# First attention: a decayed state per head in place of four of ten blocks

## The reference

```python
lam = exp2(-8 * (1..16) / 16)                      # one decay per head
scores = einsum('bhid,bhjd->bhij', q, k) * diag    # exp(-lam*(i-j)) for i >= j, else 0
o_intra = einsum('bhij,bhje->bhie', scores, v)
o_inter = einsum('bhid,bhde->bhie', q * q_dec, kv) # q_dec = exp(-lam*(r+1))
kv = exp(-lam*CHUNK) * kv + einsum('bhjd,bhje->bhde', k * k_dec, v)
o = o_intra + o_inter
```

## Time and profile before

| | us |
|---|---|
| median of 3 runs | 4115.63 (4114.98 to 4118.08) |
| the profiled execution's own time | 4116.67 |
| its span, first to last instruction | 4114.9 |
| PE busy | 3815.0 (93%) |
| DVE busy | 2393.4 (58%) |
| ACT busy | 1449.7 (35%) |
| POOL busy | 1332.2 (32%) |

### The profile page before, as it was taken

One profiled execution on the slowest core, in us unless ns is written; L12 is line 12 of the kernel. 1 busy time (PEld: TensorE's weight loads), 2 busy tenths in 40 slices (PEclk: granted clock), 3 DMA queues, 4 the chain that ended last, 5 costly groups with the idle time before them and its releaser, 6 DMA issues. The chain is left out here.

```text
span 4114.9 us, 51894 instructions
## 1 busy us (share of the span) xinstructions
PE 3815.0 (93%) x19048; PEld 2746.2 (67%) x19048; DVE 2393.4 (58%) x3950; ACT 1449.7 (35%) x2205; POOL 1332.2 (32%) x1674
## 2 busy tenths in 40 slices
PE   6877999999999999999999999999999999978678
PEld 5755777677767776677767776677767776664423
DVE  5644556555654666556654666456654665465347
ACT  4422342424243433424242433334242433314124
POOL 2421452235312541235313541244213541121114
PEclk9989999999999999999999999999999999987789
DMA  6456533254424433254324533354324433332304
GB/s 234 171 186 245 189 133 139 83 196 158 144 68 179 164 133 127 86 215 147 129 88 154 181 116 135 105 202 138 123 98 180 164 126 105 113 105 73 133 12 153
DMA packets 173802, 579.03 MB, mean 141 GB/s; under 512 B 14728, under 2 KB 14984, under 8 KB 168175
## 3 DMA queue, kind: packets, MB, share of 16 engines
q1 hardware_dynamic: 169854, 568.37, 38.8%
q10 hardware_dynamic: 3696, 7.34, 0.5%
HBM read 490.19 MB, written 84.93 MB: 140 GB/s over the span
## 5 line engine op out<-in xcount | busy, mean ns | idle before, releaser
L1776 PE MATMUL ps_P<-XnT_hi,w_ring 128*128 128x512 f32 x3328 | 1079.6, 406 | 51.6 <-DVE silu L1445 25.7
L1776 PEld LDWEIGHTS ps_P<-XnT_hi,w_ring 128*128 128x128 f32 x3328 | 610.0, 191 | 215.2 <-issue 76.2
L1776 PE MATMUL ps_P<-XnT_lo,w_ring 128*128 128x512 f32 x1664 | 659.0, 396 | 0.0
L1435 DVE TENSOR_REDUCE row_max<-ps_T 128x2 fp32r<-128x768 f32 (+3 forms) x448 | 399.3, 915 | 248.8 <-PE ps_T L1932 238.7
L833 POOL TENSOR_TENSOR pT_lo<-pf,pT_hi 128x512 fp32r<-128x512 f32 x320 | 410.8, 1291 | 303.7 <-ACT pT_hi L971 299.2
L1085 ACT ACTIVATE probs<-ps_E 128x1024 f32<-128x1024 f32 x320 | 327.1, 1022 | 393.2 <-PE ps_E L1947 393.2
L909 POOL TENSOR_TENSOR hT_lo<-hf,hT_hi 128x512 fp32r<-128x512 f32 x128 | 164.3, 1284 | 921.1 <-ACT hT_hi L971 921.1
L851 POOL TENSOR_SCALAR_AFFINE_SELECT probs<-probs 128x512 f32<-128x512 f32 x256 | 159.5, 635 | 652.1 <-ACT probs L1085 651.1
L1776 PEld LDWEIGHTS ps_P<-XnT_lo,w_ring 128*128 128x128 f32 x1664 | 317.6, 191 | 71.4
L1776 PE MATMUL ps_Y<-w_big,hT_hi 128*128 128x512 f32 x896 | 331.5, 416 | 23.0 <-POOL hT_lo L909 11.0
L824 POOL TENSOR_TENSOR sines<-swapped,sinT 128x512 f32<-128x512 f32 x160 | 213.2, 1332 | 348.7 <-ACT swapped L971 342.8
(11 more groups left out here) (307 smaller groups left out, 7263.5 us busy)
## 6 DMA issues: line engine op xcount, KB each, us to landing
w_ring<-split_dram SPq DMA_DIRECT2D x412, 512.0 KB, 3.4
w_big<-split_dram SPq DMA_DIRECT2D x64, 2048.0 KB, 7.8
dec<-decay SPq DMA_DIRECT2D x32, 1024.0 KB, 4.9
split_dram<-w_ring SPq DMA_DIRECT2D x58, 512.0 KB, 4.3
split_dram<-w_big SPq DMA_DIRECT2D x36, 512.0 KB, 4.4
wo1w<-split_dram SPq DMA_DIRECT2D x8, 2048.0 KB, 7.5
gatew<-split_dram SPq DMA_DIRECT2D x7, 2048.0 KB, 10.9
x_dram<-X SPq DMA_DIRECT2D x8, 1024.0 KB, 5.4
```

The lines of the kernel that those rows point to most:

```text
L1435: last = dve.reduce_max(row_max[:, g % 2, block, heads_of(ns)].rearrange("p (b n) -> p b n", n=len(ns)), psT[:, :, at:at + len(ns) * w].re ...
L1776: last = pe.matmul(dst, stat[s_], mov[m_], start=first_ and k == 0, stop=last_ and k == n - 1)
```

## The change

The ten blocks of a group become six score products and a state. The first two key tiles leave the state: keys (not transposed; `keys_back` turns them back through PE) times values that were scaled by their decay to the end of tile 1 (`scaled_values`). The queries of tiles 2 and 3 are multiplied with the state (`state_product`), the decay since the boundary is applied (table `far`), and the result is added to their own blocks. Score products are regrouped: tile j with the query tiles of its own pair, two heads at a time (parts 0 and 1), and the diagonal block of the second tile for four heads (part 2). The raw weights of pass 0 are staged in other memory, and the pieces of the group's output weights are split at other places. The decay table keeps its size.

```diff
+NJOB, NRING, SCORES, INTER = 10, 8, range(2, 8), (8, 9)
+def score_job(k): return divmod(k - SCORES[0], 3)
+P_F = {k: n for n, k in enumerate((0, 1, 2, 3, 4, 5, "state", 6, 7, 8, 9, "sum0", "sum1"))}
+P_HI = {k: n for n, k in enumerate((0, 1, 2, 3, "state", 4, 5, 6, 7, 8, 9))}
+UNIT_AT, KEYS_AT = (0, 1, 2, 3, 5), 4
-            out["blk", g, k + (2 if g == 0 else 7)] = [("w", BIG_O + g, k)]
+            out["blk", g, k] = [("w", BIG_O + g, k)]
...
 # ScalarE, rope, after the loop over u
+                act.wait_ge(*proj.need(n, g, KEYS_AT))
+                copy(kv[0][:, :], ps["Y0"][:, :]).then_inc(*rope_hi.hit(n, g, KEYS_AT))
                 rope_high(n, g, NU - 1)
+            def values_high(n, t):
+                act.wait_ge(*vals.need(n, t))
+                if t < 2:
+                    if t == 0 and n >= 2:
+                        act.wait_ge(*x3_out.need(n - 2))
+                    copy(v32[:, t, :], ps[YB[t % 2]][:, :])
+                copy(v[0][:, t, :], ps[YB[t % 2]][:, :]).then_inc(*v_hi.hit(n, t))
             def blocks(n, g):
+                for k in range(NJOB):
+                    if k == 4:
+                        act.wait_ge(*pv.need(n, g, 1))
+                        copy(kv[0][:, :], ps[PB[g % 2]][:, :]).then_inc(*p_hi.hit(n, g, P_HI["state"]))
+                    if k == 6 and g == 0:
+                        values_high(n, 2)
+                        values_high(n, 3)
+                    if k == 7:
+                        ...
+                        act.wait_ge(*pv.need(n, g, 4))
+                        for h in range(2):
+                            copy(oT[0][:, 2 * h:2 * h + 2, 0:2 * P], ps[EB[h]] ...).then_inc(*o_hi.hit(n, g, h))
+                    if k < NRING: ... copy(pT[0][:, k % 4, :], pf[:, k % 2, :]) ...
+                    else: ... wait sum{h}; copy(oT[0][:, 2 * h:2 * h + 2, 2 * P:4 * P], pf[:, k % 2, :]) ...
+                    if n == 0 and k >= 6:
+                        first(("blk", g, k - 6))
 # VectorE
             def blocks(n, g):
+                for k in range(2):
+                    if g == 0:
+                        values_low(n, k)
+                    scaled_values(n, g, k)         # pf <- v32 * k_dec, both in SBUF
+                if g:
+                    accumulate(n, g - 1, 0)
+                    accumulate(n, g - 1, 1)
                 dve.wait_ge(*dec_in.need(n, g))
+                for k in range(2, 6):
+                    scaled_scores(n, g, k)         # pf <- bank T * dec; waits for p_lo of job k-2
+                    if g == 1 and n:
+                        measure_pc(n - 1, k - 2)
+                dve.wait_ge(*p_hi.need(n, g, P_HI["state"]))
+                low(kv[1][:, :], ps[PB[g % 2]][:, :], kv[0][:, :]).then_inc(*p_f.hit(n, g, P_F["state"]))
+                for t in range(2, NT):
+                    accumulate(n, g - 1, t) if g else values_low(n, t)
+                for k in (6, 7):
+                    scaled_scores(n, g, k)
+                    if n == 0 and k == 6:
+                        first(("blk", g, 0))
+                for h in range(2):
+                    dve.wait_ge(*o_hi.need(n, g, h))
+                    low(oT[1] of heads 2h, 2h+1, tiles 0 and 1, ps[EB[h]] ...).then_inc(*o_lo.hit(n, g, h))
+                if n == 0:
+                    first(("blk", g, 1))
+                for k in INTER:
+                    scaled_scores(n, g, k)
+                for h, k in enumerate(INTER):
+                    dve.wait_ge(*pv.need(n, g, NRING - 1))
+                    dve.tensor_tensor(pf[:, k % 2, :], ps[EB[h]][:, :], pf[:, k % 2, :], ALU.add) ... sum{h}
+                    if n == 0:
+                        first(("blk", g, 2 + h))
 # TensorE
+            def keys_back(n, g):
+                pe.wait_ge(*rope_lo.need(n, g, 0))
+                dst = fill("Y0", rope_hi.need(n, g, KEYS_AT))
+                for t in range(2):
+                    for s_ in range(2):
+                        last = pe.matmul(dst[:, cols(2 * t + s_)], kT[s_][:, cols(t)], identr[:, :], start=True, stop=True)
+                last.then_inc(*proj.hit(n, g, KEYS_AT))
+            def state(n, g):                       # 2 tiles x 3 matmuls 128x512 into PB[g % 2]
+            def score_product(n, g, k):            # 3 matmuls 128x512
+            def value_product(n, g, k):            # parts 0, 1: 3 of 128x512 into EB[part], filled
+                dst = fill(EB[part], p_f sum{part} if pair else o_lo.need(n, g, part))
+                ...                                # part 2: 6 of 128x256, 3 into each of E0 and E1
+            def state_product(n, g, k):            # 6 matmuls 128x256 into TB[k % 2]
             def blocks(n, g):
                 pe.wait_ge(*rope_lo.need(n, g, NU - 1))
+                for k in range(2, 6):
+                    score_product(n, g, k)
+                if g == 0:
+                    all_values(n, 2)
+                state(n, g)
+                if g == 0:
+                    all_values(n, 3)
+                else:
+                    output(n, g - 1, 2)
+                    output(n, g - 1, 3)
+                value_product(n, g, 2)
+                value_product(n, g, 3)
+                score_product(n, g, 6)
+                score_product(n, g, 7)
+                value_product(n, g, 4)
+                for k in INTER:
+                    state_product(n, g, k)
+                for k in range(5, 8):
+                    value_product(n, g, k)
 # TensorE, the main loop
                         for u in range(NU):
                             project(n, g, u)
+                            if u == 3:
+                                keys_back(n, g)
...
-                            for t in range(NT):
+                            for t in range(2):
                                 all_values(n, t)
```

More of the change, by code:

```diff
@@ L175 @@
 assert len(PIECES) == NUNITS == len(set(PIECES))
+MOVED = sum(len(at) for key, at in FIRST.items() if key[0] != "slot")
 INDEX = {p: r for r, p in enumerate(PIECES)}
@@ L694, in _ @@
                         big(n, BIG_O + g)
-                        for k in range(NBLK + LAG + 1):
+                        for k in range(4):
                             if n == 0:
@@ L1524, in _ @@
                                     measure_qb(c, t)
[L1525 to L1526 removed]
+                            if c >= 0:
+                                for t in range(NT):
                                     norm("qb", c, t, y_acc[:, t, :], y_acc[:, t, :])
[L1528 to L1532 removed]
                         blocks(n, g)
@@ L1775, in product @@
                     for s_, m_ in ((0, 0), (1, 0), (0, 1)):
-                        last = pe.matmul(dst, stat[s_], mov[m_], start=first_ and k == 0, stop=last_ and k == n - 1)
+                        last = pe.matmul(dst, stat[s_], mov[m_], start=first_ and k == 0, stop=last_ and k == n - 1, **kw)
                         k += 1
@@ L1826, in output @@
                     big_ready(n, BIG_O + g)
-                pe.wait_ge(*o_lo.need(n, g, t))
+                pe.wait_ge(*(o_lo.need(n, g, 1) if t < 2 else p_lo.need(n, g, INTER[1])))
                 dst = fill(YB[t % 2], wo_acc.need(n, g, t))
                 product(dst[:, :], [(halves(oT, h, cols(t)), big_w(WB, h)) for h in range(HG)]).then_inc(*wo.hit(n, g, t))
+            def score_product(n, g, k):
+                pair, part = score_job(k)
+                dst = fill(TB[k % 2], p_f.need(n, g, P_F[k]))
+                at = slice(2 * pair * P, 2 * (pair + 1) * P) if part < 2 else cols(2 * pair + 1)
+                h = heads_of_part(part)
+                product(dst[:, :].rearrange("p (h i) -> p h i", h=h.stop - h.start),
+                        [(halves(kT, cols(2 * pair + part // 2)), halves(qT, h, at))]).then_inc(*score.hit(n, g, k - 2))
@@ new lines, in state @@
+            def state(n, g):
+                dst = fill(PB[g % 2], p_f.need(n, g, P_F["state"]))
+                keys = kv[0][:, :].rearrange("p (t s d) -> p t s d", t=2, s=2)
+                for t in range(2):
+                    pe.wait_ge(*p_lo.need(n, g, t))
+                    product(dst[:, :], [([keys[:, t, s_, :] for s_ in range(2)], halves(pT, t, slice(None)))], t == 0, t == 1)\
+                        .then_inc(*pv.hit(n, g, t))
+            def value_product(n, g, k):
+                pair, part = score_job(k)
+                j = 2 * pair + part // 2
+                if g == 0:
+                    pe.wait_ge(*v_lo.need(n, j))
+                pe.wait_ge(*p_lo.need(n, g, k))
+                stat, mov = halves(v, j, cols(g)), halves(pT, k % 4, slice(None))
+                if part < 2:
+                    dst = fill(EB[part], p_f.need(n, g, P_F[f"sum{part}"]) if pair else o_lo.need(n, g, part))
+                    last = product(dst[:, :], [(stat, mov)], True, False, skip_group_check=True)
+                else:
+                    for h in range(2):
```

(12 more changed lines are left out.)

202 lines of the change are left out of this document (105 added, 97 removed).

## The result

The changed kernel takes 4206.2 us (median of 4, 4198.8 to 4208.8) against 4116.9 beside it: ratio 1.0214, interval 1.0197 to 1.0232. The forecast was 4135 with a range to 4160. The direction held; the size did not: 89 us instead of 18.

A forecast was written before the change was run, and what follows sets the result against it. PE, busy 93% of the span, was taken to bound the kernel. From 4116.7 us, the walks gave -5.5 and falls of the clock +24: 4135, slower; range 4100 to 4160.

The forecast's parts named there:

- The matmul count: PE's matmul slots per group: 36.0 us after the change, 2.1 us less per group, 67 us over 32 groups.
- the new wait: Before output 0 of the previous group, PE waits for ACT's copy emptying bank Y0, 2.8 us.
- T: The end of projection 4 on PE, from which the prediction counts times within a group.
- the walk of all three kinds of group: Queue-by-queue timing: group 0 27.75 us against 28.79, group 1 +0.2 against 40.85, steady group 40.25 against 40.18.
- The clock: PE's granted clock falls behind the new gaps: 21 x 0.6 x 1.4 plus 7 x 0.8 x 1.2, +24 us, bounds 0 to 45.
- with no falls: Rival at the gap before output 0: clock stays at 2.4 GHz, not slower, 4111 us; chance 0.25.
- The next group's first sine waits for its swap until 30.5: just covered: At a steady group's end, POOL's last low halves end about 30.6 us from T; +1.0 us if they push that sine.
- The rival that named POOL: POOL's last two low halves push the next group's sines: +1.0 us in 28 groups, all falls, 4169 us; chance 0.15.
- The moves of the decay load and the prefetches cost nothing: The next group's whole projection phase covers them: a 1 MB load against 25 us until first use.
- If I were wrong about Y0: Without the bank wait, PE would stand before job 2's decay instead; the group would win back only about 0.5 us.
- Scaled values: DVE jobs reading two SBUF tiles: 0.69 us each in steady groups, 1.1 and 1.27 in group 0.
- Sequence 0: Pass 0, with weight splits moved and later constants: taken as 0 us, bounds -15 and +12.

The follow-up runs named there:

- e9_noclock: Changed kernel with POOL's four norms behind group 2's rotation and unread matmuls filling the gaps before output 0 and group 0's score 4: 4129.0 us, ratio 1.0014.
- e1_pool: Changed kernel with POOL's four norms moved from behind group 1's blocks to behind group 2's rotation: 4164.3 us, ratio 1.0105.
- e2_bank: Changed kernel with the transposed keys in bank O instead of Y0: 4177.6 us, ratio 1.0144.
- e3_busy: Changed kernel with 11 unread matmuls on PE before output 0 of the previous group, in groups 1 to 3: 4159.3 us, ratio 1.0091.
- e10_bo: Changed kernel with keys in bank O and output 2 (group 0: value tile 2) between scores 3 and 4, norms unmoved: 4070.5 us, ratio 0.9878.
- e7_pbod: Changed kernel with the three edits of e6_pbo plus the decay table's new address from e5_dec: 4033.1 us, ratio 0.9794.
- e6_pbo: Changed kernel with POOL's norms behind group 2's rotation, keys in bank O, output 2 (value tile 2) between scores 3 and 4: 4042.0 us, ratio 0.9815.
- e5_dec: Changed kernel with the decay table at another address, so group 0's load need not wait for the gates' store: 4201.2 us, ratio 1.0201.

## Why the forecast was wrong

**The matmul count and the new wait: right.** PE goes on at T+2.74 for 2.81. `e9_noclock` shows the walk of all three kinds of group within 0.4 us, once clock and norms are taken out; the saving was in fact spent at the bank and in the chain of jobs. Part of the fit is luck: for group 1 the walk had 0.9 us of waiting before the last value, where the changed kernel's profile lists none (over 0.15 us), and 1.2 before scores 4 and 5, where it lists 0.6.

**The clock: the mechanism right, the term mis-sized.** I took 21 gaps x 0.6 falls x 1.4 us, and 7 x 0.8 x 1.2, +24. In the changed kernel the clock fell behind 20 of those 21 gaps and in all 7 groups 0: 27 falls for 18. It also fell 13 times more where I had counted none: 5 behind POOL's gap in group 2, 4 in sequence 0, and 4 behind a gap of 2.30 us far from the change, which had 3 falls in 7 before and 7 in 7 after. So 40 more falls rather than 18, at 1.6 us (group 1, 42.31 against 40.71) to 1.8 rather than 1.2 to 1.4: some 64 to 72 us for 24. The share of 3 in 7 was carried over from one place of the kernel. The Trainium skill (TensorE: Matmul & The Clock Gate, section Why this matters for your kernels) warns of gaps in which TensorE idles between bursts of matmuls, but only of longer ones than these; the measurement differs, and it decides (20 falls behind 21 gaps of 2.59 us). Nor did the length of the gap alone tell whether the clock fell: behind 2.59 us it fell in 7 of 7 group 1s and 1 of 7 group 2s of `e1_pool`, behind 1.9 us in 21 of 21 of `e2_bank`. What decides stays open. The sum has one slip: with no falls it gives 4111, so its own range should have begun there and not at 4118.

**"The next group's first sine waits for its swap until 30.5: just covered": wrong for group 2.** I walked POOL to its last low half (30.6 from T), against the swap at 30.5, and left out what stands behind it in POOL's queue after group 1: four norms, 3.1 us (43.14 in `e3_busy` against 40.00 in `e9_noclock`, and 40.47 against 37.36 in `e10_bo`). The rival that named POOL had its place right and its price and its group wrong: nothing in groups 1 and 3, 3.1 us in group 2, plus the falls that followed. Moving four small norms past one function was worth 42 us. Before the change the norms lay in POOL's slack (2.09 us were left of it behind them); now POOL's last job is a low half of the outputs, which ends when the swap is done.

**"The moves of the decay load and the prefetches cost nothing": wrong for group 0.** The cover named, "the whole projection phase", is there for groups 1 to 3. Group 0's load waits for the store of the gates, is issued at 1882.80 and lands by 1887.9, and two value tiles that had hidden it now stand behind the scores. DVE waited for it in all six of sequences 2 to 7, 15.4 us in sum. Price: 9 us or more (`e7_pbod` against `e6_pbo`), and 5 us, not told from nothing, while PE's order keeps the other wait (`e5_dec`). Group 0 came out at +11 over seven sequences, its falls included, instead of -1.0 each; its gap was 4.8 to 7.2 for 3.7.

**"If I were wrong about Y0": right in kind.** `e2_bank` moved the gap to score 4 (1.9 us; forecast: PE would stand there) and won 1.0 us of waiting in a group (forecast 0.5). But "The result does not hang on that one wait" hid the better reading: both gates opened at once give about 3 us a group without any fall (37.36 in `e6_pbo` against 40.71 and 40.00 in `e9_noclock`).

**Scaled values:** 0.684 us in steady groups, 1.18 and 1.79 in group 0 of sequence 4 (taken: 0.69, then 1.1 and 1.27). DVE's two sums took 0.686 each, as taken.

**Sequence 0:** +11 us, inside the bounds of -15 and +12 but at their end. I have not taken it apart. Groups 1 and 2 have 2.1 to 2.2 of it each, and with the bank gap filled (`e3_busy`) 0.1 and -0.5, so there it is the fall; some 7 lie in and behind group 3.

The sum, from the forecast: 4135 + 40 to 48 (falls) + 22 (norms, 7 x 3.1) + 6 (sequence 0, from `e9_noclock`) gives 4203 to 4211, against 4206. It closes better than its terms are known: three falls of sequence 0 are in it twice, and the late load of group 0 is not in it. The falls are counted in one profiled execution of each kernel.

## What to carry over

Where a wait is walked to be "just covered" on an engine, read that engine's queue to its next wait, with the small instructions of other parts of the kernel in it. A saving behind two gates in a row shows in full only when both are open, so try the edits together before one is given up as worthless. And an idle gap of PE such as these (1.9 to 7.2 us) is priced as its length plus up to one fall of the clock, 1.6 to 1.8 us here; matmuls nobody reads, put into the gap, measure the second part by itself.

## What the hardware showed unexpectedly

- Filling 24 gaps with 11 matmuls each, without moving a wait, took 26 falls of the clock away and made the kernel 47 us faster.
- The same 2.30 us gap in an untouched part of the kernel fell 3 times of 7 before and 7 of 7 after (3 to 7 of 7 in the other kernels): falls there varied with no edit near.
- The same 1 MB load took 4.7 to 8.4 us from issue to landing in the 32 groups of the changed kernel, median 4.9. In group 0 of sequence 2 its reader started 6.1 us after the issue (946.39 to 952.50), in sequence 4 5.1.
